# Two layers of attention on one core: PSUM banks moved from the transposed scores to the scan

## The reference

```python
# layer 0
mod = silu(condition) @ Wada + bada                  # six rows of 256 for each image
xm = layernorm(x) * (1 + sc_a) + sh_a
x = x + gt_a * proj(softmax(causal(q k^T * hd**-0.5)) v)
xm = layernorm(x) * (1 + sc_m) + sh_m
x = x + gt_m * (gelu(xm @ W1 + b1) @ W2 + b2)
# layer 1, no causal mask
h1 = x + proj(softmax(q k^T) / D**0.5 @ v)           # q, k, v of a modulated layernorm of x
out = sln(h1) + h1
```

## Time and profile before

| | before |
|---|---|
| median of 3 runs | 1492.99 us (1488.58 to 1497.8) |
| profiled execution | 1490.63 us |
| its span | 1488.8 us |
| mean granted TensorE clock | 0.931 of 2.4 GHz |
| PE, matmuls busy | 1272.3 us (85%) |
| DVE busy | 867.4 us (58%) |
| ACT busy | 676.0 us (45%) |
| POOL busy | 244.0 us (16%) |

### The profile page before, as it was taken

How to read it: one execution, slowest core, us unless ns; L and a number is a source line. 1 busy time by engine, 2 the same in 40 slices (tenths; PEclk the granted TensorE clock), 3 DMA queues, 4 the chain that set the end, 5 groups by cost and what they waited for, 6 DMA issues and landing times.

```text
span 1488.8 us, 19068 instructions
## 1 busy us (share of the span) xinstructions
PE 1272.3 (85%) x7004; PEld 601.1 (40%) x7004; DVE 867.4 (58%) x1741; ACT 676.0 (45%) x1328; POOL 244.0 (16%) x257
## 2 busy tenths in 40 slices
PE   2589589999989998999889989999899988995881
PEld 0234254445434544445434543454444442442111
DVE  3262356774687468755876468737875576415711
ACT  0116104564465455465446445545546544550360
POOL 4101200120033002210122003200221020102002
PEclk9659789999999999999999999999999998997686
DMA  6401504140425115240515051502423152005002
GB/s 195 85 16 15 116 1 100 18 114 2 101 52 109 23 36 117 46 86 13 126 32 113 2 115 37 124 8 51 102 48 84 15 123 46 1 8 129 1 2 51
DMA packets 59278, 91.63 MB, mean 62 GB/s; under 512 B 12240, under 2 KB 23072, under 8 KB 59184
## 3 DMA queue, kind: packets, MB, share of 16 engines
q1 hardware_dynamic: 58320, 89.61, 27.0%
q10 hardware_dynamic: 864, 0.79, 0.2%
HBM read 25.57 MB, written 4.77 MB: 20 GB/s over the span
## 4 chain that ended last, share of the span: by engine, by line
PE 62%; DVE 18%; issue 6%; DMA 4%; ACT 4%; SPq 3%; POOL 1%; ACTq 0%; POOLq 0%; DVEq 0%
PE SX L786 11%; PE DN L825 11%; PE OP L761 11%; PE SC L773 10%; DVE MX L604 8%; PE DN L863 7%; PE DN L846 7%; DVE STAT L611 2%; DMA OC<-OE 2%; PE SX L789 2%; PE DN L836 1%; ACT E L487 1%; PE SC L776 1%; DVE XN L647 1%; DVE XR L699 1%
## 5 line engine op out<-in xcount | busy, mean ns | idle before, releaser
L604 DVE TENSOR_REDUCE MX<-SX 128x1 f32<-128x512 f32 (+3 forms) x1024 | 556.9, 585 | 293.8 <-PE SX L789 199.6
L487 ACT ACTIVATE E<-SC 128x512 f32<-128x512 f32 (+3 forms) x1024 | 469.2, 521 | 377.1 <-PE SC L773 195.3
L786 PE MATMUL SX<-KS,QS 96*128 96x512 bf16 (+3 forms) x1024 | 329.9, 365 | 94.3 <-DVE MX L604 68.9
L773 PE MATMUL SC<-QS,KS 99*128 99x512 bf16 (+3 forms) x1024 | 298.4, 352 | 17.8 <-ACT E L487 9.0
L761 PE MATMUL OP<-E,V 128*32 128x512 f32 (+3 forms) x2048 | 236.4, 533 | 1.1 <-ACT E L487 1.1
L773 PEld LDWEIGHTS SC<-QS,KS 99*128 99x128 bf16 x1024 | 97.4, 98 | 286.2 <-ACT E L487 182.2
L786 PEld LDWEIGHTS SX<-KS,QS 96*128 96x128 bf16 x1024 | 100.1, 100 | 241.4 <-DVE MX L604 161.6
L863 PE MATMUL DN<-XT,W 128*128 128x512 f32 x256 | 123.0, 606 | 2.7 <-ACT HID L527 1.8
L407 POOL TENSOR_TENSOR RSTD<-VE,HALF 128x4 f32<-128x4 f32 x32 | 32.5, 1017 | 561.6 <-DVE VE L616 561.6
L846 PE MATMUL DN<-XT,WQKV 128*128 128x512 f32 x256 | 119.9, 612 | 2.8 <-DVE X L661 1.7
L825 PE MATMUL DN<-W,HID 128*128 128x256 f32 x512 | 117.2, 382 | 0.0
(11 more groups left out here) (89 smaller groups left out, 980.6 us busy)
## 6 DMA issues: line engine op xcount, KB each, us to landing
QS<-PART SPq DMA_DIRECT2D x96, 256.0 KB, 5.3
KS<-PART SPq DMA_DIRECT2D x96, 256.0 KB, 7.4
OC<-OE SPq DMA_DIRECT2D x64, 128.0 KB
RB<-recip_sums SPq DMA_DIRECT2D x64, 128.0 KB, 2.6
XIN<-in_x SPq DMA_DIRECT2D x8, 512.0 KB, 9.5
ROW<-row_vectors SPq DMA_DIRECT2D x8, 512.0 KB, 3.9
out<-OUT SPq DMA_DIRECT2D x8, 512.0 KB, 2.9
W<-in_w SPq DMA_DIRECT2D x2, 1024.0 KB, 12.5
```

The costliest lines, as they stand in the source:

```text
L487: a.activation(E[:, at["step"].index() % 2, j, lo:T], SC[(4 * s + j) % 3][:, lo:T], ACT.Exp, scale=HD ** -0.5 if attend == 0 else 1.0)\
L604: v.reduce_max(MX[:, qt, h:h + 1], SX[at["scan"].index() % 2][:, 0:w], AX.X, negate=True)\
L773: ins = t_.matmul(SC[u % 3][:, lo:T], KS[attend][0:ALL_ROWS, h, kt * P:kt * P + P], QS[attend][0:ALL_ROWS, h, lo:T], start=True, stop=atte ...
L786: ins = t_.matmul(bank[:, 0:w], QS[layer][0:CUT_ROWS, h, qt * P:qt * P + P], KS[layer][0:CUT_ROWS, h, 0:w], start=True, stop=layer == 1)
```

## The change

The scan gets a third bank and the transposed scores lose one. The index of each bank and the number in each wait follow from that: a scan waits for the maximum of the scan three before, a transposed score for the exponential of the score two before. The third modulation product at the start of the kernel goes to the first SX bank. Order, operands and all other instructions stay.

```diff
-        SC = [pb(f"SC{i}", [P, T]) for i in range(3)]
+        SC = [pb(f"SC{i}", [P, T]) for i in range(2)]
         DN = [pb(f"DN{i}", [P, T]) for i in range(2)]
-        SX = [pb(f"SX{i}", [P, T]) for i in range(2)]
+        SX = [pb(f"SX{i}", [P, T]) for i in range(3)]
...
-                        a.activation(E[:, at["step"].index() % 2, j, lo:T], SC[(4 * s + j) % 3][:, lo:T],
+                        a.activation(E[:, at["step"].index() % 2, j, lo:T], SC[(4 * s + j) % 2][:, lo:T],
...
-                then(v.tensor_tensor(MODS[:, c * T:c * T + T], SC[c][0:B, :], VEC[:, c * T:c * T + T], ALU.add))
+                then(v.tensor_tensor(MODS[:, c * T:c * T + T], (SC + SX)[c][0:B, :], VEC[:, c * T:c * T + T], ALU.add))
...
-                v.reduce_max(MX[:, qt, h:h + 1], SX[at["scan"].index() % 2][:, 0:w], AX.X, negate=True)\
+                v.reduce_max(MX[:, qt, h:h + 1], SX[at["scan"].index() % 3][:, 0:w], AX.X, negate=True)\
...
-                    ins = t_.matmul(SC[c][0:B, :], CS[:, k, :], WADA[:, k, c * T:c * T + T],
+                    ins = t_.matmul((SC + SX)[c][0:B, :], CS[:, k, :], WADA[:, k, c * T:c * T + T],
...
-                wait(pe, exp_done, at["head"].at(1, j if u == 0 else j - 2))
-                ins = t_.matmul(SC[u % 3][:, lo:T], KS[attend][0:ALL_ROWS, h, kt * P:kt * P + P],
+                wait(pe, exp_done, at["head"].at(1, j if u == 0 else j - 1))
+                ins = t_.matmul(SC[u % 2][:, lo:T], KS[attend][0:ALL_ROWS, h, kt * P:kt * P + P],
                                 QS[attend][0:ALL_ROWS, h, lo:T], start=True, stop=attend == 1)
                 if attend == 0:
-                    ins = t_.matmul(SC[u % 3][:, lo:lo + P], ID16[:], CAUSAL_T[:], start=False, stop=True)
+                    ins = t_.matmul(SC[u % 2][:, lo:lo + P], ID16[:], CAUSAL_T[:], start=False, stop=True)
...
-                bank = SX[at["scan"].index() % 2]
-                wait(pe, scan_done, at["scan"].at(1, -1))
+                bank = SX[at["scan"].index() % 3]
+                wait(pe, scan_done, at["scan"].at(1, -2))
```

## The result

| | before | after |
|---|---|---|
| median | 1490.78 us (4 runs) | 1613.5 us (4 runs, 1609.42 to 1614.23) |
| ratio | 1 | 1.082 (95% interval 1.0784 to 1.0857) |
| span of the profiled execution | 1488.8 us | 1612.4 us |
| mean granted clock | 0.931 | 0.913 |

The change makes the kernel 122.7 us slower. The forecast was 82 us (1575 us); the time lies in the range, near the figure of case 2 (1620 us).

What follows compares the result with a forecast made beforehand. PE was taken to set the time, with DVE doing so in places. New score stalls of 171.7 us less 89.5 us of scan waits gave +82 us on the profiled 1490.63, so a median of 1575 us, range 1530 to 1640.

Steps and rivals of the forecast that it cites:

- case 2: DVE's lags behind its chunk work don't shrink, so half of the 89.5 us stays: 1620 us, chance 0.18.
- The new stall: Score 2 of every "a" waits for score 0's exponential: 89.6 us layer 1, 71.4 layer 0, 10.7 ahead of up_3.
- the two steps that were computed singly: Score 2 behind score 0: 1.13 us in a layer 1 "a", 2.5 us in the "a" ahead of up_3.
- I bound the two together by the whole of today's scan waits: Third scan bank and later TensorE together give back all scan waits on DVE: 68.9 + 20.6 = 89.5 us.
- The sum has no term for it: Short stalls don't lower TensorE's clock, as a steady pass with 13 scan waits shows 0.99; nothing was added.
- Case 3: Clock falls to 1.2 GHz more often, seven full passes at 0.96 from 0.99, losing 34 us: 1609 us, chance 0.09.
- case 1: The forecast itself: new score stalls less the scan waits given back, 1575 us, chance 0.64.
- The signs to look for: Line 773's ACT waits 100 us or more, line 786's below 20, pass about 171 us, chain moving to ACT's exponentials.
- The threshold for case 2: Line 786's scan waits for DVE staying above 35 us would show case 2 right.
- That for case 3: The windows' clock in the steady passes falling below 0.97 would show case 3 right.
- Cases 4 and 5: Faster, stalls falling into waits for DVE: 1404 us, chance 0.04; no measurable change, 1480 to 1505 us, chance 0.05.

Runs made afterwards that it cites:

- e3: Changed kernel with the third score (score 2) of each "a" moved behind the PV, same banks (two score, three scan): 1520.77 us.
- e9: e1 plus one unused matmul of 512 columns between scores 1 and 2 of every "a", into the unused bank: 1615.16 us.
- e1: Changed kernel with the scan back on two banks, scores on two, one PSUM bank unused: 1637.32 us, ratio to before 1.0989.
- e6: Kernel before with one bank for dense work in place of two, the spare bank unused: 1724.55 us.
- e7: e6 with the spare bank given to the scan, so three banks for scores and three for the scan: 1702.64 us.

## Why the prediction came out as it did

**The new stall: right.** 171.7 us were summed from rows, 169.2 us were measured between the scores' starts, and the two steps that were computed singly (1.13 us and 2.47 us) came out to the hundredth. That the sum agrees is partly luck: the place behind max0b (1.81 us and not 0.87) was missed. e3 confirms the cause: the same banks with score 2 elsewhere are 92.7 us faster. What the stalls cost in time is less than their sum. e9 has as much time at 1.2 GHz as the kernel before (206 and 207 us): its scores 0 to 2 lie 167.1 us further apart, its scan waits are 24.5 us shorter (with 0.16 us for each), and it is 125.9 us slower and not 142.6. About 17 us of its stalls cost nothing; no run shows where.

**"I bound the two together by the whole of today's scan waits": mis-sized.** The step took 89.5 us for given back, on the argument that a later TensorE and one more bank together exceed the median wait. The waits lost 64.6 us. Long ones stay in part (3.7 us the longest, 3.9 before), and e1 against the changed kernel and e6 against e7 put the bank's own part at 24 and 22 us of time. That part is case 2's mechanism, at a smaller size than the 45 us it was given.

**"The sum has no term for it" (the clock): wrong.** By estimate it is worth about 22 us: the time at 1.2 GHz rose by 74 us with the change (207 to 281), and the filler of e9, which took 22 us off, lowered it by 72 (278 to 206). The steady pass shown at 0.99 before did hold 13 short waits; with a stall in every "a", one of them of 1.88 us, the first six full passes hold 48 us at 1.2 GHz where they held 10. The Trainium skill, "TensorE: Matmul & The Clock Gate", section on PSUM-queue depth-cycling, tells of a kernel that cycles through PSUM banks and whose TensorE idles briefly and often between groups of matmuls, so that the clock swings between its levels. The time at 1.2 GHz in e1 and e9 agrees with it. Case 3's mechanism was at work beside case 1's, at two thirds of its 34 us. Case 3 also took all seven full passes to stand at 0.99 before; the seventh stood at 0.87 already. Treating the clock as a rival, and not as a term, was the mistake.

**Together:** 169.2 - 64.6 + 22 = 126.6 us against 122.7 measured. That this comes within 4 us is luck. The same sum for e1 is 165.9 - 25.8 + 22 = 162 us, and 147.5 were measured; from e1 to the changed kernel the scan's waits fall by 38.7 us, and the time by 24. The two misses, of some 15 us each, have opposite signs: the stalls and the waits both count for less in time than in the lists of waits.

The signs to look for were mostly met: line 773's waits above 100 us, the chain's move to ACT, line 786's below 20 us. The pass came to 174.4 us and not 171. The threshold for case 2 (waits of line 786 above 35 us) said no. That for case 3 (steady passes below 0.97) was crossed by one of the first six full passes, at 0.96, and not by the other five, 0.97 to 0.99. Parts of both cases were true, and about half of the clock's growth lay outside the passes that the threshold looked at. Thresholds for a rival as a whole miss one that is there in part. Cases 4 and 5 were out; no step shows a stall that fell wholly into a wait for DVE.

## What to carry to other kernels

Count the banks of a producer against its longest run of items without other work between them: here a third item behind two banks waited for one full round trip (landing, reader, release), whatever the average load said, while the producer whose items come in pairs got only 22 to 24 us from a third bank. Where banks serve two kinds of work in a fixed order, try one ring in place of a split: here the same five gave 1465 us against 1490, and the same four 1560 against 1637. Price a wait by a run that removes it, not by its length: a removed scan wait gave about half of itself. And where a change adds a short standstill of TensorE in every step, put a term for the clock in the sum.

## What was not expected of the hardware

Matmuls that nobody needs made a kernel faster: 256 of them, of 512 columns each, took 22 us off 1637 us, with the time at 1.2 GHz down from 278 to 206 us. A standstill of 1.88 us, at the same place in each of seven passes, was followed by a fall of the clock in four of them and by none in three: four matmuls took 3.14 us in one pass and 1.88 us in another.
